# Convolution part of a one-core hybrid kernel: filter rows on GpSimd, a five-bank ring, moved variance, whole transposes, residual on VectorE

## What is computed

```
x = x + conv(_gn(x))                      # depthwise, 51 x 51 filter, padding 25
t = tokens(x)                             # 16 x 256 x 32
t = t + attention(_ln_t(t))               # sparse mask gated by a spiking recurrence over time
t = t + steps(_ln_t(t))                   # up to 33 steps, attention or FFN, chosen by the data
```

## Time and profile before

| quantity | value |
|---|---|
| median of three runs | 219.69 us (218.63 to 220.36) |
| the profiled execution, its own time | 218.97 us |
| its span (first to last instruction) | 217.2 us |
| mean granted TensorE clock | 0.906 of full speed |
| TensorE busy / VectorE / ScalarE / GpSimd | 79% / 66% / 50% / 27% |
| the convolution part, up to the first residual on VectorE | 0 to 39.0 us |
| chain that ended last, by engine | PE 55%, DVE 19%, ACT 8%, issue 8% |

### The profile page before, as it was taken

One profiled execution on the slowest core, in us unless ns is written; L12 is line 12 of the kernel. 1 busy time (PEld: TensorE's weight loads), 2 busy tenths in 40 slices (PEclk: granted clock), 3 DMA queues, 4 the chain that ended last, 5 costly groups with the idle time before them and its releaser, 6 DMA issues.

```text
span 217.2 us, 4109 instructions
## 1 busy us (share of the span) xinstructions
PE 171.0 (79%) x1197; PEld 116.4 (54%) x1199; DVE 142.4 (66%) x392; ACT 107.8 (50%) x318; POOL 58.3 (27%) x136
## 2 busy tenths in 40 slices
PE   8589969965594799989369499999684999998730
PEld 5554856532392577745242278677332787765310
DVE  0862265857957688893844478898755589787452
ACT  2334261237853566662577058676441576755330
POOL 8800000000060545561000004654600036555100
PEclk9999999999769589999956969999997599999985
DMA  6500000000000000000000000000000000000002
GB/s 210 199 0 3 0 3 1 2 0 5 0 0 0 3 0 3 0 0 0 10 11 6 18 0 0 0 0 0 0 0 14 0 0 0 0 0 0 0 0 98
DMA packets 2635, 3.18 MB, mean 15 GB/s; under 512 B 825, under 2 KB 1849, under 8 KB 2618
## 3 DMA queue, kind: packets, MB, share of 16 engines
q1 hardware_dynamic: 2330, 2.66, 3.9%
q10 hardware_dynamic: 288, 0.32, 0.5%
HBM read 2.45 MB, written 0.53 MB: 14 GB/s over the span
## 4 chain that ended last, share of the span: by engine, by line
PE 55%; DVE 19%; ACT 8%; issue 8%; DMA 3%; POOL 3%; DVEq 2%; ACTq 1%; SPq 1%; POOLq 0%
PE bank L502 15%; PE bank L475 8%; PE bank L489 4%; PE bank L466 4%; PE bank L728 4%; ACT qz L890 3%; PE bank L562 3%; PE bank L616 3%; PE bank L545 3%; DVE big L1168 3%; POOL prob L418 3%; DMA kx<-kx_dram 2%; DVE minus L1152 2%; DVE filt L331 2%; PE bank L766 2%
## 5 line engine op out<-in xcount | busy, mean ns | idle before, releaser
L418 POOL TENSOR_SCALAR prob<-prob,einv 128x256 f32<-128x256 f32 x96 | 44.9, 482 | 62.6 <-DVE einv L1163 62.6
L1168 DVE COPY big<-bank 128x512 f32<-128x512 f32 x48 | 32.9, 686 | 6.2 <-PE bank L475 6.1
L475 PE MATMUL bank<-ident,prob 128*128 128x128 f32 x192 | 31.2, 286 | 6.9 <-POOL prob L418 6.8
L807 ACT ACTIVATE prob<-bank,nmax 128x256 f32<-128x256 f32 x64 | 29.8, 472 | 12.8 <-DVE nmax L1155 12.8
L502 PE MATMUL bank<-hT,qz 128*128 128x256 f32 x128 | 33.6, 391 | 0.0
L475 PEld LDWEIGHTS bank<-ident,prob 128*128 128x128 f32 x192 | 22.2, 144 | 19.5 <-POOL prob L418 15.3
L502 PEld LDWEIGHTS bank<-hT,qz 128*128 128x128 f32 x128 | 23.2, 198 | 4.1 <-issue 1.6
L1155 DVE TENSOR_REDUCE nmax<-bank 128x2 f32<-128x512 f32 x32 | 21.7, 687 | 5.1 <-PE bank L502 4.6
L807 ACT ACTIVATE prob<-minus,nmax 128x256 f32<-128x256 f32 x32 | 15.9, 499 | 10.9 <-DVE nmax L1152 8.3
L502 PE MATMUL bank<-kt,qz 128*128 128x256 f32 x64 | 18.4, 419 | 3.2 <-ACT prob L807 3.2
L545 PE MATMUL bank<-ident,filt 128*128 128x128 f32 x96 | 12.2, 276 | 5.1 <-DVE big L1003 2.1
(11 more groups left out here) (161 smaller groups left out, 253.6 us busy)
## 6 DMA issues: line engine op xcount, KB each, us to landing
xrev<-xrev_dram SPq DMA_DIRECT2D x1, 512.0 KB, 5.3
xin<-xtok_dram SPq DMA_DIRECT2D x1, 512.0 KB, 5.2
out_dram<-outT SPq DMA_DIRECT2D x2, 256.0 KB, 2.3
wx<-wx_dram SPq DMA_DIRECT2D x1, 288.0 KB, 4.0
maskc<-maskc_dram SPq DMA_DIRECT2D x1, 256.0 KB, 4.9
kx<-kx_dram ACTq DMA_DIRECT2D x1, 248.0 KB, 4.1
constf<-constf_dram SPq DMA_DIRECT2D x1, 218.0 KB, 5.3
wa<-wa_dram SPq DMA_DIRECT2D x3, 56.0 KB, 1.8
```

Source lines behind the costliest of these rows:

```text
L418: last = nc.gpsimd.tensor_scalar(prob[b % NPB][:, ih, :], prob[b % NPB][:, ih, :], einv[:, b, ih:ih + 1], 1.0, ALU.mult, ALU.mult)
L475: mm = pe.transpose(bank[2 + b % 2][:, jh * S + ih * P:jh * S + (ih + 1) * P], prob[b % NPB][:, ih, jh * P:(jh + 1) * P], ident)
L807: e = nc.scalar.activation(prob[b % NPB][:, ih, :], scores, ACT.Exp, bias=nmax[:, b, ih:ih + 1], scale=-1.0 if masked else 1.0, accum_out= ...
L1168: nc.vector.tensor_copy(flat(probT[b % NTB]), bank[2 + b % 2][:, :]).then_inc(s_PT, 1)
```

## The change

It does the following, all in the part up to the first LayerNorm:

- VectorE makes the filter rows of chunk 0 only, GpSimd those of chunks 1, 2 and 3.
- The loads: `ident` goes first on SyncE's queue, `wx` is split in two (chunk 0, then the rest), `kx` is alone on ScalarE's queue. `constf` is smaller, as `pick` is gone.
- The ring of the Toeplitz blocks has five banks for chunks 0 to 2 and four for chunk 3; `TOEP` shares the copies out anew (14 on ScalarE, 10 on VectorE).
- The squares' sums stand ahead of T(2), and `pairs` ahead of C(1). ScalarE loads the table for the root at the start, by a one-element root.
- C(j) no longer waits for a bank except at j = 2. `CDRAIN` gives each group its own engine and signal: groups 0, 1, 4, 6 ScalarE, 2, 3, 5, 7 VectorE. VectorE's scaling of group 5 stands ahead of its 15 small instructions, that of group 7 behind them.
- `to_tokens` transposes whole 128 x 128 blocks of `convr` (of each 128 columns 64 are wanted and 64 come along, so a half takes two banks), and VectorE reads the wanted ones with a step of 32 elements.
- The product with `xin` is gone; VectorE adds `xin` for half 1 too. ScalarE's copy of half 1 of `tok` is gone.

```diff
+        TBANK = [(0, 1, 5, 7, 6)[n % 5] for n in range(3 * NT)] + [(0, 1, 5, 7)[n % 4] for n in range(NT)]
+        STATS = 4
+        CBANK = (2, 2, 3, 3, 2, 3, 0, 1)
+        CDRAIN = "AADDADAD"
+        TOKENS = (4, 6)
...
+        TOEP = "AADADA" + "ADAADA" + "ADADAD" + "ADADAD"
+        CONVT = "DD"
...
-            sp.dma_start(flat(wx[:, :, :, :]), d["wx"]).then_inc(s_wx, 16)
+            sp.dma_start(ident, d["identf"]).then_inc(s_id, 16)
+            sp.dma_start(flat(wx[:, 0:1, :, :]), d["wx"][:, 0:NQ * HW]).then_inc(s_wx0, 16)
+            sp.dma_start(flat(wx[:, 1:, :, :]), d["wx"][:, NQ * HW:]).then_inc(s_wx, 16)
...
-            for ck in (2, 3):
+            for ck in (1, 2, 3):
                 filter_rows(ck, pool, nc.gpsimd.tensor_tensor, s_filtP)
...
-                if j >= 2:
-                    pe.wait_ge(s_convA if j % 2 == 0 else s_convD, 1)
+                if j == 2:
+                    for who, s in (("A", s_convA), ("D", s_convD)):
+                        pe.wait_ge(s, count(who, CDRAIN[:4]))
...
             def to_tokens(j):
 
-                pe.wait_ge(s_convA if j % 2 == 0 else s_convD, j // 2 + 1)
+                for who, s in (("A", s_convA), ("D", s_convD)):
+                    wait(pe, s, 0, count(who, CDRAIN[:2 * j + 2]))
                 for h in range(NH):
                     for cg in (2 * j, 2 * j + 1):
-                        mm = pe.matmul(st.bank(K_CONVT + h)[:, cg * GB * B:(cg + 1) * GB * B], convr[:, cg, h * P:(h + 1) * P], pick,
-                                       start=(h == 0 and cg == 0), stop=(cg == CG - 1))
+                        mm = pe.transpose(psum[:, TOKENS[h] * 512 + cg * P:TOKENS[h] * 512 + (cg + 1) * P],
+                                          convr[:, cg, h * P:(h + 1) * P], ident)
...
-            pe.wait_ge(s_xin, 16)
-            pe.matmul(st.bank(K_CONVT + 1)[:, :], ident, xin[:, 1, :, :].rearrange("p b c -> p c b"), start=True, stop=False)
...
+            act.wait_ge(s_zero, 2)
+            nc.scalar.activation(table[:, :], eps[0:1, :], ACT.Sqrt)
...
-            for ck in (0, 1):
+            for ck in (0,):
                 filter_rows(ck, dve, nc.vector.tensor_tensor, s_filtD)
...
             scale_conv(1)
             copy_toep(3)
+            scale_conv(2)
...
             def conv_residual(h):
-                conv = st.bank(K_CONVT + h)[:, :].rearrange("p (c b) -> p b c", b=B)
+                conv = psum[:, TOKENS[h] * 512:(TOKENS[h] + 2) * 512].rearrange("p (c r) -> p r c", c=C)[:, 0:B, :]
                 st.filled(dve, K_CONVT + h)
-                if h == 1:
-                    return conv
                 nc.vector.tensor_tensor(tok[:, h, :, :], xin[:, h, :, :], conv, ALU.add).then_inc(s_dd, 1)
```

More of the change, by code:

```diff
@@ L65, in constants @@
     same = (rows[:, None] // 32 == rows[None, :] // 32) & (rows[:, None] % B == rows[None, :] % B)
[L66 to L69, removed]
     stepcode = np.zeros((P, NSTEPS), np.float32)
@@ L528, in keep_clock @@
                     for i in range(SPARE):
-                        pe.matmul(bank[0], ident[:, 0:P // 2].bitcast(BF16), constf[:, 0:2 * P].bitcast(BF16), start=True, stop=True)
+                        pe.matmul(SPAREB, ident[:, 0:P // 2].bitcast(BF16), constf[:, 0:2 * P].bitcast(BF16), start=True, stop=True)
             pe.wait_ge(s_zero, 1)
@@ L538, in toeplitz @@
                     n = ck * NT + i
[L539 to L542, removed]
+                    done = 1 + group_of(4 * i + 3 + YH - 1 - 15)
+                    if ck == 0:
+                        pe.wait_ge(s_filtD, done)
+                    else:
+                        pe.wait_ge(s_filtP, NQ * (ck - 1) + done)
+                    if TBANK[n] in TBANK[:n]:
+                        last = max(m for m in range(n) if TBANK[m] == TBANK[n])
+                        pe.wait_ge(s_toepA if TOEP[last] == "A" else s_toepD, count(TOEP[last], TOEP[:last + 1]))
                     for u in range(4):
                         a0 = 4 * i + 3 - u
-                        mm = pe.transpose(bank[TBANK[n % TRING]][:, u * P:(u + 1) * P], flat(filt[:, ck, a0:a0 + YH, :]), ident)
+                        mm = pe.transpose(bank[TBANK[n]][:, u * P:(u + 1) * P], flat(filt[:, ck, a0:a0 + YH, :]), ident)
                     mm.then_inc(s_toep, 1)
@@ L561, in convolve @@
                                 left, rows = xcc[:, c, 1, :], B
-                            mm = pe.matmul(bank[CBANK[j]][q * 32:q * 32 + rows, (cg % 2) * S:(cg % 2 + 1) * S], left,
+                            mm = pe.matmul(bank[CBANK[cg]][q * 32:q * 32 + rows, (cg % 2) * S:(cg % 2 + 1) * S], left,
                                            flat(toep[:, c, (1 - hi) * YH:(3 - hi) * YH, :]), start=(hi == 0), stop=(hi == 1),
@@ L580, in _ @@
             for h in range(NH):
-                mm = pe.matmul(bank[3], ones256[:, :], flat(xrev[:, h, :, :]), start=(h == 0), stop=(h == NH - 1))
+                mm = pe.matmul(bank[STATS], ones256[:, :], flat(xrev[:, h, :, :]), start=(h == 0), stop=(h == NH - 1))
             mm.then_inc(s_mean, 1)
             toeplitz(1)
-            pe.wait_ge(s_xin, 16)
-            pe.matmul(st.bank(K_CONVT + 1)[:, :], ident, xin[:, 1, :, :].rearrange("p b c -> p c b"), start=True, stop=False)
             pe.wait_ge(s_xc, NH)
             convolve(0)
-            toeplitz(2)
             pe.wait_ge(s_sq, 2)
             for cg in range(CG):
-                mm = pe.matmul(bank[3][:, cg:cg + 1], flat(sqc[:, cg * GB:(cg + 1) * GB, :, :]), ones256[:, 0:1],
+                mm = pe.matmul(bank[STATS][:, cg:cg + 1], flat(sqc[:, cg * GB:(cg + 1) * GB, :, :]), ones256[:, 0:1],
                                start=True, stop=True)
             mm.then_inc(s_vh, 1)
-            convolve(1)
+            toeplitz(2)
             pe.wait_ge(s_vhs, 1)
             pe.wait_ge(s_cf, 16)
-            pe.matmul(bank[3][:, CG:2 * CG], pairs, vhalf[:, :], start=True, stop=True).then_inc(s_vp, 1)
+            pe.matmul(bank[STATS][:, CG:2 * CG], pairs, vhalf[:, :], start=True, stop=True).then_inc(s_vp, 1)
+            convolve(1)
             toeplitz(3)
@@ L817, in _ @@
             act.dma_start(flat(kx[:, :, :]), d["kx"]).then_inc(s_kx, 16)
-            act.dma_start(ident, d["identf"]).then_inc(s_id, 16)
             def ln_act(n, copy_tok):
@@ L833, in copy_toep @@
             def copy_toep(ck):
-                for n in range(ck * NT, (ck + 1) * NT, 2):
-                    act.wait_ge(s_toep, n + 1)
-                    dst, src = toep_block(n)
-                    nc.scalar.activation(dst, src, ACT.Copy).then_inc(s_toepA, 1)
+                for n in range(ck * NT, (ck + 1) * NT):
+                    if TOEP[n] == "A":
+                        act.wait_ge(s_toep, n + 1)
+                        dst, src = toep_block(n)
+                        nc.scalar.activation(dst, src, ACT.Copy).then_inc(s_toepA, 1)
             def scale_conv(j):
@@ L999, in copy_toep @@
             def copy_toep(ck):
-                for n in range(ck * NT + 1, (ck + 1) * NT, 2):
-                    dve.wait_ge(s_toep, n + 1)
-                    dst, src = toep_block(n)
-                    nc.vector.tensor_copy(dst, src).then_inc(s_toepD, 1)
+                for n in range(ck * NT, (ck + 1) * NT):
+                    if TOEP[n] == "D":
+                        dve.wait_ge(s_toep, n + 1)
+                        dst, src = toep_block(n)
+                        nc.vector.tensor_copy(dst, src).then_inc(s_toepD, 1)
             def scale_conv(j):
```

58 lines of the change are left out of this document (25 added, 33 removed).

## The result

| | before | changed |
|---|---|---|
| median of the first measurement | 220.01 us (4 runs) | 211.62 us (4 runs, 208.1 to 212.6) |
| ratio, first measurement | | 0.954 (95%: 0.944 to 0.964) |
| ratio, second measurement (c1 below, 6 runs) | 218.95 us | 0.963 (0.957 to 0.969), median 210.28 us |
| the profiled execution: its time, its span | 218.97, 217.2 | 208.1, 206.3 |
| mean granted clock | 0.906 | 0.901 |

The ratios leave out executions that lie over 1.5% above the fastest of their kernel and count as slow, which takes out 212.6 and 212.18 here (the 0.954 rests on 208.1, 211.05 and a fifth execution of 209.68) and two of the six in c4, but none of c1, where the fastest was less fast and executions go up to 212.89. The medians as they stand give 211.62 / 220.01 = 0.962. Both measurements say faster, by 3.1% to 5.6% with their intervals; 3.2% was forecast.

A forecast was written before the change was run, and what follows sets the result against it. TensorE's list plus 5.1 us of gaps was taken as the bound until 39 us. 7.8 us before the first residual, less 0.65 and 0.15, gave 7.0, so 219.69 - 7.0 = 212.7 us; range 210.0 to 216.5.

The forecast's parts named there:

- What bounds the part: Up to the first residual at 38.99 us: the limit is TensorE's own list plus 5.1 us of gaps.
- `toeplitz` = 2.9: TensorE's list after the change: 24 transposes for one chunk take 2.86 us by the old trace, taken as 2.9.
- the 7.0: Whole gain: 7.8 us up to the first residual, less 0.65 for the second residual and 0.15 for small waits.
- Start: First Toeplitz transposes on TensorE: they start at 5.4 us (bounds 5.3 and 5.8) instead of 6.42, 1.0 us gained.
- the floor of 5.3: TensorE's start: the warm-up products end at 5.47, the last issued a little earlier, so no start before 5.3 us.
- The gaps: TensorE's waits before the convolution's end: those of 1.25, 0.90 and 2.03 us go, 4.2 us; 0.95 at the start.
- The new wait: Ahead of the last transposes of `convr`: TensorE stands still 0.95 us, until VectorE scales group 7 at 30.7.
- Transposes: Transposes of `convr` on TensorE: 16 passes instead of 32, 2.0 us gained.
- Second residual: Half 1's addition on VectorE in the LayerNorm's chain: 0.69 us more, +0.65 with the overlap.
- The lower bound: VectorE's two additions reading PSUM with a step of 32: +0 taken, from bounds of +0 and +0.74 us together.
- GpSimd as the bound: Rival, chance 0.04: GpSimd's filter rows come too late for the last Toeplitz blocks; slower, about 223.7 us.
- The clock behind: Rival behind the changed part: TensorE's clock falls take some 3 us (214.5 to 216.5, 0.18) or give up to 2.5 (0.08).

The follow-up runs named there:

- c1: The changed kernel run again without an edit, beside the kernel before: ratio 0.963 (0.957 to 0.969), median 210.28 us; first residual at 30.97.
- c4: The changed kernel with the first six of VectorE's 15 small instructions moved ahead of its scaling of group 5: ratio 0.950 to the kernel before, median 208.8 us.
- d3: The changed kernel with the residual's product of identity and input put back: 23.48 us from the mean's first product to the last four transposes, instead of 21.76.
- r1: The changed kernel with a ring of three banks for all Toeplitz blocks: 23.34 us from the mean's first product to the last four transposes, instead of 21.76.
- d4: The changed kernel with the old loads (filter weights in one transfer, identity second on ScalarE's queue): first Toeplitz transpose at 6.12 us, first residual at 32.90.
- r3: The changed kernel with a three-bank ring and filter rows of chunks 0 and 1 on VectorE: 23.33 us from mean to last transposes, first residual at 32.13.
- r2: The changed kernel with filter rows of chunks 0 and 1 on VectorE, ring of five kept: 21.76 us from mean to last transposes, first residual at 30.91.
- r4: The changed kernel without the early one-element root, the table loaded at the variance: 21.75 us from mean to last transposes, first residual at 29.66.
- e3: The changed kernel run once more without an edit: first residual at 29.79 us, 159.2 us from the last query and key products to the end.
- d1: The changed kernel with 20 spare products in TensorE's waits between the query and key products: ratio 0.963 (0.958 to 0.969), median 209.99 us.
- d2: The changed kernel with the spare products of d1 and the edit of c4 together: ratio 0.964 (0.959 to 0.969), median 210.45 us.

## Why the prediction was right or wrong, point by point

- **What bounds the part** was right: TensorE's list and its gaps. d3 gives 1.72 back for the product that was put at 1.7 to 1.8, and the distance from the mean to the last transposes is the same to 0.02 us in every trace with the same list.
- **The term `toeplitz` = 2.9 was mis-sized.** It was read off a row of before in which the three-bank ring held some blocks for a moment. It measured 2.65 to 2.72, and 2.84 once r1 put the ring back. Three of them after T(0) make 0.65 us, the fourth 0.28 where TensorE was already fast (2.62). Of the 1.25 us by which the first trace beats the 7.0 in this part, this is 0.93, the earlier start 0.27. This is the step that failed in the convolution part.
- **Start.** `kx` landed at 3.9 (bounds 3.1 and 4.9, 4.5 taken), T(0) began at 5.13, 5.26 and 4.89 for 5.4. That T(0) starts earlier was right, but the reason was misread: it was put to `kx` and the filter rows, with `ident` "not waited for", while before the change T(0) waited for `ident` (6.4; d4 has the same wait back at 6.1). After the change neither is waited for. The time was 0.1 to 0.5 too late, and the floor of 5.3 was not one: the warm-up itself varies from 3.8 to 4.45 us. That T(0) could run at half pace (3.43 for 2.62) was not in the sum; in c1 it cancels the mis-sized term almost exactly, so that the first residual at 30.97 for a predicted 31.1 is luck; in the first trace it did not occur (30.03).
- **The gaps** went as said, but for other reasons in part: the one of 0.95 was a wait for `ident` (d4), the ring is worth 1.58 (r1), the wait in T(0) stays away with the ring and the two chunks of before (r3), the third chunk on GpSimd and the early table load give nothing (r2, r4).
- **The new wait** was right in place and cause: 0.74 for 0.95, ended by VectorE's scaling at 29.4 for 30.7; c4 removes it.
- **Transposes**: 16 for 32 passes; K(0) 0.53 us for 0.93. Right.
- **Second residual**: 0.69 and 0.68 for 0.69; a step of 32 elements from PSUM costs no more than one of 16. The lower bound was the right choice, and the rule on lines in the Trainium skill (SBUF — State Buffer, the note on cachelines) is not borne out by these two additions.
- **GpSimd as the bound**: not seen. Its 27 rows took 7.21, 0.27 each. VectorE's nine rows took 1.22 us, 0.14 each, when GpSimd was still writing zeros or waiting, against 0.22 each when both made rows; in d4, where both start at 4.8, the nine took 1.83. That gained some 0.7 us for VectorE that nothing needed. The rule on the shared read port (the Trainium skill, SBUF — State Buffer, Who interferes with whom) fits in kind, but not as a lock for whole instructions: from 5.01 to 8.99 before the change, VectorE made 18 rows (2.4 us at 0.14) and GpSimd about 14 (3.7 us at 0.27), by this estimate 6.1 us of work in 4.0.
- **The clock behind.** The mechanism was named, the side was not: I gave a loss 0.18 and a gift 0.08 and let the range end at 210.0. In the first trace it gave 2.65 of the 10.9 us; in c1 1.8 of 9.1, in e3 nothing. This is the second step that failed: over all traces the part behind varies between 156.5 and 159.2 us, and the trace of before, from which the sum starts, stands at 159.1. That left 0.1 us of loss against 2.6 of gift, where I allowed 3 of loss and let the range take in little of the gift. Whether the changed kernel has better luck on average (157.3 to 159.2 without the first trace, against 158.0 to 159.1) stays open; three traces of each don't tell.

So the sum of 7.0 stands against 7.3 (c1) to 8.5 (e3) measured in the convolution part up to `xt` (46.77 against 39.47 and 38.29), and against 8.4 and 8.7 between the medians of the two measurements. The sum was 0.3 to 1.5 us short in the part and held nothing for the clock, and the range ended 0.4 us above the time that the first ratio gives.

## What to carry to other kernels

A row without an idle time can still hold waits: where a resource is scarce in the old kernel, take the pace of an instruction from a row in which it is plentiful, and expect the pace of the scarce one to improve as well. When two rows name two releasers for one start, look up when each was done: the later one is the wait. When several edits cover the same wait, only one earns; undo them one at a time before keeping the others. And when a change moves work in front of a part whose clock falls and rises on its own, give the gain a spread to both sides as wide as that part's own spread.

## What the runs showed of the hardware that I had not expected

- In the first microseconds TensorE went at two paces, 7 and 11 instructions a microsecond, and the change between them came between 4.2 (r4) and 7.0 us (c1), once near 10 (d4), in executions of the same or nearly the same code, while the profile's granted clock read 1.00 all the time. That moved the first residual of the changed kernel by 1.2 us.
- The place where the granted clock falls moves against the work: between the first two traces the falls moved by 11.0 us, the work at the first of them by 8.24. One microsecond of later rise there went with 0.9 us at the end, in 15 traces of kernels with and without the change.
- Keeping TensorE busy where it waited removed one fall, but the next came where it cost as much (d1: 158.5 us behind the products; d2, with the same spare products: 157.5).
